# Token tiles laid down the image, with conv1, conv2 and the output transposes handed on chunk by chunk

## The chip, the core and the metric

One core of a Trainium2 chip runs the whole program in one launch. The metric is the device time in microseconds, as the median of several runs. TensorE (PE) multiplies and transposes, VectorE (DVE), ScalarE (ACT) and GpSimd (POOL) work on elements, SyncE (SP) issues the DMAs.

## The reference

Eight images x of 64 x 64 pixels and 48 channels go through four layers, all in float32:

```
L0: attention over all 4096 tokens of an image, then concat with x (96 channels),
    1x1 conv + leaky ReLU ("conv1"), 3x3 conv + leaky ReLU ("conv2"), 1x1 conv ("w3"), + x
L1: ReLU, 3x3 depthwise conv, 1x1 conv, batch norm
L2: routing (mean, 4 experts), 1x1 conv to 192 ("expand"), 3x3 depthwise, 1x1 conv to 48 ("project")
L3: as L1
```

## The kernel before

The images are pipelined. One iteration f of the loop does conv2, w3 and L1 of image f, project and L3 of image f-1 (`back`), and attention and conv1 of image f+1 (`attn`). Iterations 0 and 7 are written out, 1 to 6 are a loop, each image takes 142.3 us. Everything is ordered by hand: each engine has its own program, and semaphores tie them together. TensorE's order in an iteration is conv2, project(0), w3(3), project(1), l1(0,1), project(2,3), transposes of x, l1(2), l1(3), attention scores, routing, l3 (four chunks), attention sums, `out_tokens` (16 transposes), attention weights, halo of the expansion, and conv1 with the expansions between its chunks.

**Two layouts.** Convolutions work on "pairs": a partition holds one of 2 x 48 channels (even and odd row of a row pair), the free axis holds rows and columns; a PSUM bank is 512 elements, 8 rows of 64. Attention works on "tokens": `tok` has 128 tokens on the partitions, in 16 tiles i for each row parity. Before, tile i takes columns 16q + i (q = 0 to 3, `WQ`) of all 32 row pairs, so every token tile spans the whole height of the image. A group of four transposed tiles (a chunk of 512 tokens) is therefore four columns out of each quarter, all rows of one parity.

**conv1** runs over 8 such chunks k. TensorE transposes four tiles (L1045) and multiplies (L1053), ScalarE copies the input (L1279) and writes 0.2 times the result to y1 (L1286), VectorE takes the maximum twice: L670 into the float32r tile y1_h in image layout, and L672 back into y1. GpSimd then subtracts (L949) for y1_l, VectorE does the last chunk itself (L676). L670 reads bank and y1 in the order of the image: runs of 4 elements, 128 apart (`bank_tokens`, `y1_tokens`), and writes through `y1_view`. The two banks of ring C are freed by L672 (y1_max). In the loop an expansion (L1109, L1110) stands between conv1's chunks, whose result ScalarE (L1377) or VectorE (L648) takes.

**conv2** (L1070) does 27 matmuls for each of 8 chunks of 8 rows. Its first matmul waits for all eight y1_h chunks, its 19th for all y1_l chunks, because a chunk of tokens spans all rows.

**w3_out** (L702) adds w3's bank, a bias and x, which it reads from xcm with a stride of 128.

**l3** (L1094 to L1097) does 15 matmuls for each of four chunks, ScalarE evacuates them to outc (L1362). After the attention sums `out_tokens` transposes outc, tile i being outc[:, i::16] (L1172), and ScalarE copies four groups to ot (L1370). Ring D's two banks are taken in turn; place p waits for the reader of place p - 2.

**DMAs.** `load_x` issues 12 DMAs an image (pieces of 192 bytes), `store` 4, with runs of 3072 bytes on both sides. VectorE's depthwise convolution of an image waits until the store before has landed, since ot shares its tile.

## Time and profile before

| | us |
|---|---|
| median of 3 runs (1265.3 to 1267.52) | 1265.95 |
| the profiled run | 1266.09 |
| its span | 1264.3 |
| TensorE busy | 1175.6 |
| VectorE busy | 892.4 |
| ScalarE busy | 475.6 |
| GpSimd busy | 119.8 |

The span is that of one execution taken by the profiler. "PE" is a matmul, "PEld" a weight load beside it. In the tables of groups a row gives line, engine, operation, output and inputs, shapes, count, then busy time and mean ns, then idle time before it and what ended it. In the timeline the first two columns are start and duration in us, and the brackets hold the idle time before and its cause. Matmuls are pipelined, so one may be shown 0.4 us long while the next starts 0.24 us after it.

### The profile page before, as it was taken

The page shows a single profiled execution, that of the slowest core. Times are in us where ns is not written, and L with a number is a line of the kernel's source. Part 1 is how long each engine was busy: PE and PEld are TensorE (multiplying, and loading weights), DVE is VectorE, ACT ScalarE, POOL GpSimd, SP SyncE. Part 2 cuts the span into 40 slices and gives each one's busy share as a digit, 9 for nine tenths or more (in the row PEclk, how much of TensorE's full clock was granted, in tenths as well). Part 3 has the DMA queues.
Part 4 walks back from the last instruction along what each step waited for, and adds up shares of the span by engine and source line. Part 5 has one row for each costly group of instructions (what it writes and reads, how often), then busy time and mean ns, then how long its engine had stood idle before and what let it go on. Part 6 is the DMA issues. An engine that isn't in the chain of part 4 may idle for free.

```text
span 1264.3 us, 14703 instructions
## 1 busy us (share of the span) xinstructions
PE 1175.6 (93%) x4981; PEld 756.8 (60%) x4981; DVE 892.4 (71%) x1154; ACT 475.6 (38%) x812; POOL 119.8 (9%) x72
## 2 busy tenths in 40 slices
PE   4789879999999999999999999999999999998986
PEld 3556566646665575656665575656665575655434
DVE  4552359984699459984699459984699459982850
ACT  3211334245532444245532444245532444242421
POOL 0310003000300003000300003000300003000000
PEclk9689869999999999999999999999999999999997
DMA  2011631069113772069113771069113770069016
GB/s 52 21 36 21 81 51 38 1 85 132 45 21 40 100 103 37 0 85 131 44 21 40 100 103 37 0 85 130 45 22 40 101 103 1 1 85 134 25 27 83
DMA packets 183179, 72.91 MB, mean 58 GB/s; under 512 B 174349, under 2 KB 174962, under 8 KB 183154
## 3 DMA queue, kind: packets, MB, share of 16 engines
q1 hardware_dynamic: 183154, 72.58, 41.6%
q8 instruction: 15, 0.25, 0.1%
q14 instruction: 10, 0.08, 0.0%
HBM read 10.51 MB, written 6.29 MB: 13 GB/s over the span
## 4 chain that ended last, share of the span: by engine, by line
PE 80%; DVE 7%; issue 4%; ACT 3%; SPq 2%; DMA 2%; POOL 0%; ACTq 0%; DVEq 0%; POOLq 0%
PE bank L1070 32%; PE bank L1094 8%; PE bank L1024 4%; PE bank L1081 4%; PE bank L1053 4%; PE bank L1160 3%; PE bank L1161 3%; PE bank L1013 3%; DVE dwa L632 3%; PE bank L1097 3%; PE bank L1096 3%; PE bank L1109 2%; PE bank L1138 2%; PE bank L1110 2%; DMA y_parts<-a_parts 2%
## 5 line engine op out<-in xcount | busy, mean ns | idle before, releaser
L1070 PE MATMUL bank<-y_parts,w_h 96*96 96x512 f32 x1152 | 301.8, 411 | 0.0
L632 DVE SCALAR_TENSOR_TENSOR dwa<-h1a,dyn,dwa 128x1024 f32<-128x1024 f32 x240 | 294.0, 1278 | 0.0
L1070 PEld LDWEIGHTS bank<-y_parts,w_h 96*96 96x96 f32 x1152 | 186.6, 163 | 98.5 <-issue 13.2
L632 DVE SCALAR_TENSOR_TENSOR dwb<-h1b,dyn,dwb 128x1024 f32<-128x1024 f32 x128 | 154.9, 1278 | 0.0
L1070 PE MATMUL bank<-y_parts,w_l 96*96 96x512 f32 x576 | 147.9, 401 | 0.0
L1094 PE MATMUL bank<-a_parts,wt_h 128*96 128x512 f32 x384 | 117.4, 415 | 16.4 <-DMA y_parts<-a_parts 15.9
L1070 PEld LDWEIGHTS bank<-y_parts,w_l 96*96 96x96 f32 x576 | 93.4, 162 | 44.3
L949 POOL TENSOR_TENSOR y_parts<-y,y_parts 96x512 fp32r<-96x512 f32 x56 | 96.4, 1725 | 190.5 <-DVE y L672 189.0
L943 POOL TENSOR_TENSOR tok<-tok,u 128x1536 f32<-128x1536 f32 x8 | 22.4, 2796 | 747.3 <-DVE u L573 747.3
L1094 PEld LDWEIGHTS bank<-a_parts,wt_h 128*96 128x96 f32 x384 | 61.5, 166 | 49.6 <-issue 18.7
L713 DVE SCALAR_TENSOR_TENSOR a_parts<-v,a_parts 96x512 fp32r<-96x512 f32 x64 | 43.5, 688 | 52.4 <-ACT a_parts L1339 49.6
L1053 PE MATMUL bank<-xq,w_cur 97*96 97x512 f32 x128 | 69.5, 625 | 9.7 <-DVE y L672 9.7
L670 DVE TENSOR_TENSOR y_parts<-bank,y 96x512 fp32r<-96x512 f32 x64 | 68.5, 1071 | 7.6 <-ACT y L1286 6.7
L1311 ACT ACTIVATE y<-bank,b2s 96x512 f32<-96x512 f32 x32 | 21.9, 683 | 136.3 <-PE bank L1070 136.3
L1311 ACT ACTIVATE xq<-bank,b2s 96x512 f32<-96x512 f32 x32 | 21.9, 685 | 130.9 <-PE bank L1070 122.0
L1024 PE MATMUL bank<-tok 128*97 128x48 f32 x512 | 55.0, 277 | 15.6 <-POOL tok L943 15.6
L1160 PE MATMUL bank<-dwa,pc 128*96 128x512 f32 x128 | 65.4, 592 | 0.0
L1161 PE MATMUL bank<-dwb,pc 128*96 128x512 f32 x128 | 65.3, 592 | 0.0
L1024 PEld LDWEIGHTS bank<-tok 128*97 128x97 f32 x512 | 55.0, 196 | 16.9 <-issue 16.0
L726 DVE TENSOR_TENSOR y_parts<-y,y_parts 96x512 fp32r<-96x512 f32 x32 | 22.1, 689 | 50.8 <-ACT y_parts L1352 50.8
L1094 PE MATMUL bank<-a_parts,wt_l 128*96 128x512 f32 x192 | 57.8, 410 | 0.0
L1362 ACT ACTIVATE dwa<-bank,conv_bias,inv 96x512 f32<-96x512 f32 x32 | 24.8, 774 | 81.4 <-PE bank L1097 81.4
(223 smaller groups left out, 1701.6 us busy)
## 6 DMA issues: line engine op xcount, KB each, us to landing
y_parts<-a_parts SPq DMA_DIRECT2D x32, 396.0 KB, 6.1
y_parts<-a_parts SPq DMA_DIRECT2D x64, 192.0 KB, 6.6
tok<-in_x_dram SPq DMA_DIRECT2D x96, 96.0 KB, 2.6
a_parts<-a_parts SPq DMA_DIRECT2D x32, 264.0 KB, 3.3
x_even<-y_parts SPq DMA_DIRECT2D x16, 384.0 KB, 9.0
x_odd<-y_parts SPq DMA_DIRECT2D x16, 384.0 KB, 7.9
out_dram<-dwb SPq DMA_DIRECT2D x32, 192.0 KB, 2.3
y_parts<-a_parts SPq DMA_DIRECT2D x32, 132.0 KB, 4.3
```

Of the source, the lines that this page charges most:

```text
L632: nc.vector.scalar_tensor_tensor(out=dst, in0=tap_input(n, t), scalar=weight, in1=dst, op0=ALU.mult, op1=ALU.add).then_inc(tap_step, 1)
L670: nc.vector.tensor_tensor(y1_view(y1_h, k - 1), bank_tokens(bank), y1_tokens(k - 1), ALU.max).then_inc(y1h_ready, 1)
L713: return nc.vector.scalar_tensor_tensor(out=lo[:, rows, 1:W + 1], in0=src[:, m % 2, :].rearrange("p (j w) -> p j w", w=W), scalar=0.0, in1 ...
L949: nc.gpsimd.tensor_tensor(y1_view(y1_l, k), y1_tokens(k), y1_view(y1_h, k).bitcast(F32), ALU.subtract).then_inc(y1l_ready, 1)
L1024: last = nc.tensor.matmul(bank[0:SUMS, 0:C], token(par, i, X_AT, SUMS), token(par, i, K_AT, C), start=first, stop=final)
L1053: nc.tensor.matmul(bank[0:C2, :], w1_cur[:, :], xq[:, (k - 1) % 2, :], start=True, stop=True)\
L1070: last = nc.tensor.matmul(bank[0:C2, :], wgt[:, t, :], src[:, rows, cols], start=t + n == 0, stop=t == TAPS - 1 and n == 2)
L1081: last = nc.tensor.matmul(bank[0:C2, :], w3eo[:, par, :], rows[:, :, par, :], start=par == 0, stop=par == 1)
L1094: nc.tensor.matmul(bank[0:C2, :], wgt[layer][:, kw, :], own[:, rows, kw:kw + W], start=n + kw == 0, stop=False)
L1160: nc.tensor.matmul(bank[0:C2, :], pc[:, 0, cols], first[:, :, par, :], start=False, stop=False)
L1161: last = nc.tensor.matmul(bank[0:C2, :], pc[:, 1 + m // 2, cols], other[:, :, par, :], start=False, stop=par == 1)
L1311: nc.scalar.activation(y2[(k // 2) % 2][:, (k % 2) * BANK:(k % 2 + 1) * BANK], ring_c.bank(C_2 + k)[0:C2, :], ACT.Identity, bias=b2s[:, 0: ...
```

## The change

The token tiles are laid out differently: tile i takes rows 4i to 4i + 3, all 64 columns, two row pairs (`STEP` = 2) by 64 columns on 128 partitions. Four tiles of one parity are then eight rows of that parity, and four tiles of pairs are exactly one bank of the pair layout. From this follow:

- L670, L676, L949 and L702 read and write plain rows; the gather patterns go. VectorE no longer waits for L670 before L672.
- conv1's chunk k is parity k % 2 of rows 16(k // 2) to 16(k // 2) + 15, so rows are finished from the top.
- conv2's chunk k waits for y1_h and y1_l of chunks up to k + 1 only. ScalarE, which writes y2 over y1 at k = 2, waits there for all low parts.
- `out_tokens` transposes tile by tile the chunk that l3 has made. TensorE's order is l3(0), l3(1), out(0), l3(2), out(1), l3(3), out(2), attention sums, out(3). Ring D's places follow: l3 has 4, 5, 7, 9, the transposes 6, 8, 10, 11. ScalarE copies in the same order.
- `load_x` is 6 DMAs of 64 partitions, `store` 4 DMAs of 64 partitions; both sides of each in pieces of 192 bytes (48 channels of one pixel).

The diff, with what is left out marked:

```diff
-WQ = 4
-RUN = W // WQ
+STEP = 2
+RUN = PAIRS // STEP
-X_LOADS = 3 * WQ
+X_LOADS, STORES = 3 * STEP, 2 * STEP
...
-        D_P, D_L3, D_OUT = 0, 4, 8
+        D_P, D_L3, D_OUT = 0, (4, 5, 7, 9), (6, 8, 10, 11)
         ring_d = Ring(banks[6:8], [(ah3_ready, PCHUNKS, n + 1) for n in range(PCHUNKS)]
-                      + [(outc_ready, PCHUNKS, n + 1) for n in range(PCHUNKS)]
-                      + [(ot_ready, 4, n + 1) for n in range(4)], first_free=True)
+                      + [(outc_ready, PCHUNKS, 1), (outc_ready, PCHUNKS, 2), (ot_ready, 4, 1), (outc_ready, PCHUNKS, 3),
+                         (ot_ready, 4, 2), (outc_ready, PCHUNKS, 4), (ot_ready, 4, 3), (ot_ready, 4, 4)], first_free=True)
...
         def y1_tokens(k):
 
-            return columns(y1[:, :, :], (k % Y1_BUFFERS) * BANK, [[WQ, PAIRS], [1, WQ], [128, 4]])
-
-        def bank_tokens(bank):
-            return columns(bank, 0, [[WQ, PAIRS], [1, WQ], [128, 4]])
+            return y1[:, k % Y1_BUFFERS, :].rearrange("p (j w) -> p j w", w=W)
 
         def y1_view(tile, k):
 
-            par, i0 = k // 4, 4 * (k % 4)
-            return columns(tile[:, :, :], (1 + par) * WP + 1 + i0, [[2 * WP, PAIRS], [RUN, WQ], [1, 4]])
+            r0 = 1 + 2 * ROWS * (k // 2) + k % 2
+            return tile[:, r0:r0 + 2 * ROWS - 1:2, 1:W + 1]
...
-                    nc.vector.tensor_tensor(y1_view(y1_h, k - 1), bank_tokens(bank), y1_tokens(k - 1), ALU.max).then_inc(y1h_ready, 1)
-                    dve.wait_ge(y1h_ready, CHUNKS * image + k)
+                    nc.vector.tensor_tensor(y1_view(y1_h, k - 1), bank.rearrange("p (j w) -> p j w", w=W), y1_tokens(k - 1), ALU.max).then_inc(y1h_ready, 1)
...
-                x_in = columns(xcm[0:C2, :], m * ROWS * WQ, [[1, ROWS * WQ], [128, RUN]])
                 nc.vector.scalar_tensor_tensor(
-                    out=v[:, m % 2, :].rearrange("p (a b) -> p a b", b=RUN),
-                    in0=ring_b.bank(B_W3 + m)[0:C2, :].rearrange("p (a b) -> p a b", b=RUN),
-                    scalar=col0[:, Z_B3:Z_B3 + 1], in1=x_in, op0=ALU.add, op1=ALU.add).then_inc(v_ready, 1)
+                    out=v[:, m % 2, :], in0=ring_b.bank(B_W3 + m)[0:C2, :], scalar=col0[:, Z_B3:Z_B3 + 1],
+                    in1=xcm[0:C2, m * BANK:(m + 1) * BANK], op0=ALU.add, op1=ALU.add).then_inc(v_ready, 1)
...
-            for n in range(2 * WQ):
-                par, q = n % 2, n // 2
-                sp.dma_start(tok[q::WQ, par, :, X_AT:X_AT + C], src[par, q]).then_inc(x_loaded, 16)
-            for q in range(WQ):
-                sp.dma_start(tok[q::WQ, 1, :, Q_AT:Q_AT + C], src[0, q]).then_inc(x_loaded, 16)
+            for par, at, of in ((0, X_AT, 0), (1, Q_AT, 0), (1, X_AT, 1)):
+                for j in range(STEP):
+                    sp.dma_start(tok[j * W:(j + 1) * W, par, :, at:at + C], src[of, j]).then_inc(x_loaded, 16)
...
-            dst = out[image].rearrange("(j b) (q i) c -> q j b (i c)", b=2, q=WQ)
-            for q in range(WQ):
-                sp.dma_start(dst[q], ot[q::WQ, :].rearrange("p (b n) -> p b n", b=2)).then_inc(stored, 16)
+            dst = out[image].rearrange("(i j b) w c -> j b w i c", j=STEP, b=2)
+            for j in range(STEP):
+                src = ot[j * W:(j + 1) * W, :].rearrange("p (b i c) -> p b i c", b=2, c=C)
+                for par in range(2):
+                    sp.dma_start(dst[j, par], src[:, par]).then_inc(stored, 16)
...
-                        par, i0 = k // 4, 4 * (k % 4)
+                        par, i0 = k % 2, 4 * (k // 2)
...
-                        if k == 0 and n == 0:
-                            pe.wait_ge(y1h_ready, CHUNKS * image + CHUNKS)
-                        if k == 0 and n == 2:
-                            pe.wait_ge(y1l_ready, POOL_CHUNKS * image + POOL_CHUNKS)
+                        if n == 0 and k + 2 <= CHUNKS:
+                            pe.wait_ge(y1h_ready, CHUNKS * image + k + 2)
+                        if n == 2 and k + 2 <= POOL_CHUNKS:
+                            pe.wait_ge(y1l_ready, POOL_CHUNKS * image + k + 2)
+                        if n == 2 and k + 2 == CHUNKS:
                             pe.wait_ge(y1l_last, image + 1)
...
-            def out_tokens(image):
-                for n in range(4):
-                    bank = ring_d.take(pe, image, D_OUT + n)
-                    if n == 0:
-                        pe.wait_ge(outc_ready, PCHUNKS * image + PCHUNKS)
+            def out_tokens(image, chunks):
+                for n in chunks:
+                    bank = ring_d.take(pe, image, D_OUT[n])
+                    pe.wait_ge(outc_ready, PCHUNKS * image + n + 1)
                     for m in range(4):
                         i = 4 * n + m
-                        last = nc.tensor.transpose(bank[:, m * C2:(m + 1) * C2], outc[:, i::RUN], ident[0:C2, 0:C2])
+                        last = nc.tensor.transpose(bank[:, m * C2:(m + 1) * C2], outc[:, i * 128:(i + 1) * 128], ident[0:C2, 0:C2])
                     last.then_inc(outt_done, 1)
...
+            def l3_and_out(image):
+                l3(image, (0, 1))
+                for m in range(2, PCHUNKS):
+                    out_tokens(image, (m - 2,))
+                    l3(image, (m,))
+                out_tokens(image, (PCHUNKS - 2,))
...
+                    if k == 2:
+                        act.wait_ge(y1l_ready, POOL_CHUNKS * (f + 1))
+                        act.wait_ge(y1l_last, f + 1)
...
+            def l3_and_tokens_out(b, chunks):
+                for m in chunks:
+                    l3_out(b, (m,))
+                    tokens_out(b, (m - 1,))
...
                 if back is not None:
-                    l3_out(back, (0, 1))
+                    l3_out(back, (0,))
+                    l3_and_tokens_out(back, (1,))
                 if attn is not None:
                     root_of_q(attn)
                 if back is not None:
-                    l3_out(back, (2, 3))
-                    tokens_out(back)
+                    l3_and_tokens_out(back, (2, 3))
+                    tokens_out(back, (PCHUNKS - 1,))
```

## Rows read from the trace of the kernel before

**Rows 1.** The page, busy time of each engine.
```profile
PE 1175.6 (93%) x4981; PEld 756.8 (60%) x4981; DVE 892.4 (71%) x1154; ACT 475.6 (38%) x812; POOL 119.8 (9%) x72
```
**Rows 2.** Waits of TensorE, 205 to 1145: total us, times, longest.
```profile
PE bank L1159 <- ACT dwa L1302: 7.6, 7, 1.2
```
**Rows 3.** Groups by line and form, VectorE.
```profile
L670 DVE TENSOR_TENSOR y_parts<-bank,y 96x512 fp32r<-96x512 f32 x64 | 68.5, 1071 | 7.6 <-ACT y L1286 6.7
L672 DVE TENSOR_TENSOR y<-bank,y 96x512 f32<-96x512 f32 x64 | 44.0, 687 | 2.2
...
L702 DVE SCALAR_TENSOR_TENSOR v<-bank,col,xcm 96x512 f32<-96x512 f32 x32 | 35.7, 1117 | 11.5 <-PE bank L1081 11.5
...
L690 DVE SCALAR_TENSOR_TENSOR y<-bank,col,y 96x512 f32<-96x512 f32 x32 | 23.8, 745 | 20.6 <-ACT y L1311 20.6
```
**Rows 4.** Stages, conv1: length, busy PE, PEld, DVE, ACT, POOL, granted clock, DMA.
```profile
467.40:488.88 21.48, 19.99 (x88) 12.09 (x86) 17.56 (x25) 13.45 (x25) 11.54 (x7) 1.00 0.19 55
```
**Rows 5.** Timeline, TensorE in the conv1 stage of that image.
```profile
476.41 1.09 PE L1053 MATMUL bank<-xq,w_cur 97*96 97x512 f32 x2 [0.38 <-DVE y L672]
...
485.71 1.09 PE L1053 MATMUL bank<-xq,w_cur 97*96 97x512 f32 x2 [0.70 <-DVE y L672]
...
488.72 2.38 PE L1070 MATMUL bank<-y_parts,w_h 96*96 96x512 f32 x9
```
**Rows 6.** Chain that ended last, one chunk of that stage: start, us, what.
```profile
478.41 0.86 PE bank L1053 x2
479.27 0.24 PE bank L1109
479.51 0.23 PE bank L1110
479.75 0.44 PE bank L1045 x4
```
**Rows 7.** Timeline, output transposes of that image, and those of the tail.
```profile
464.80 2.35 PE L1172 MATMUL bank<-ident,dwa 96*128 96x96 f32 x16
...
465.12 0.20 DVE L597 TENSOR_TENSOR gm<-bank,gram_mask 97x48 f32<-97x48 f32 x1
...
467.07 0.37 PE L1032 MATMUL bank<-wva_aug,gt 97*48 97x96 f32 x2
...
1256.71 2.37 PE L1172 MATMUL bank<-ident,dwa 96*128 96x96 f32 x16 [0.96 <-ACT dwa L1362]
```
**Rows 8.** Timeline, from w3 of the last pair to project(2).
```profile
551.20 1.09 DVE L702 SCALAR_TENSOR_TENSOR v<-bank,col,xcm 96x512 f32<-96x512 f32 x1 [1.23 <-PE bank L1081]
...
563.62 0.47 PE L1159 MATMUL bank<-x_even,pick 96*96 96x512 f32 x1 [1.09 <-ACT dwa L1302]
```
**Rows 9.** Timeline, TensorE in the prologue.
```profile
17.84 2.47 PE L1001 MATMUL bank<-ident,tok 128*96 128x128 f32 x10 [2.88 <-DMA tok<-in_x_dram]
...
56.39 1.10 PE L1053 MATMUL bank<-xq,w_cur 97*96 97x512 f32 x2 [0.63 <-DVE y L672]
...
63.60 1.10 PE L1053 MATMUL bank<-xq,w_cur 97*96 97x512 f32 x2 [0.76 <-DVE y L672]
...
68.64 0.79 PE L990 MATMUL bank<-col,h1a 48*96 48x1 f32 x4 [3.45 <-DVE colm L509]
...
69.36 4.16 PE L1070 MATMUL bank<-y_parts,w_h 96*96 96x512 f32 x9
```
**Rows 10.** Stages as above: first load, then SBUF copies; last, DMA share and GB/s.
```profile
9.00:17.00 8.00, 3.05 (x12) 1.98 (x12) 3.33 (x17) 0.00 (x0) 0.00 (x0) 1.00 0.75 145
446.00:458.00 12.00, 12.00 (x52) 8.17 (x51) 11.22 (x22) 6.38 (x8) 2.80 (x1) 1.00 1.42 143
```
**Rows 11.** Timeline, the end of the last iteration and the last store.
```profile
1215.41 2.25 ACT L1302 ACTIVATE dwa<-dwa 128x1024 f32<-128x1024 f32 x2 [1.76 <-DVE dwa L632]
...
1220.15 0.80 PE L1159 MATMUL bank<-x_even,pick 96*96 96x512 f32 x1
...
1259.69 2.52 SPq L870 DMA_DIRECT2D out_dram<-dwb  x4
```

More of the change, by code:

```diff
@@ L621, in depthwise @@
                     if s == 0:
-                        after(dve, stored, 16 * WQ * image)
+                        after(dve, stored, 16 * STORES * image)
                         dve.wait_ge(h1b_ready, H1B_WRITES * (image + 1))
@@ L1082, in w3, with pair_conv @@
                 last.then_inc(w3_done, 1)
-            def pair_conv(image, layer, ring, first, done, chunks):
+            def pair_conv(image, layer, ring, places, done, chunks):
                 for m in chunks:
-                    bank = ring.take(pe, image, first + m)
+                    bank = ring.take(pe, image, places[m])
                     if m % 2 == 0:
@@ L1176, in l1, with l3 @@
                 pair_conv(image, L1, ring_b, B_L1, l1_done, chunks)
[L1178 to L1179 removed]
+            def l3(image, chunks):
+                pair_conv(image, L3, ring_d, D_L3, l3_done, chunks)
+            def l3_and_out(image):
[4 more added lines that the diff above has]
+                out_tokens(image, (PCHUNKS - 2,))
             def iteration(f, attn, back):
```

31 lines of the change are left out of this document (15 added, 16 removed).

## The prediction

> **What bounds the kernel now.** I read the page first: TensorE is busy 93% of the span, VectorE 71% [rows 1]. So the kernel is TensorE's queue, and only two things can move the time: TensorE idling less, or the head and tail where no matmul runs. The waits of TensorE inside the loop come next. From 205 to 1145 us, six and a half images, the largest is 7.6 us for a ReLU that closes a depthwise chain [rows 2]; the next ones are in conv1, 0.38 and 0.70 us in the image read here, for VectorE's second max L672 [rows 5]. Then the timeline of one image (142.3 us) by stages. In conv1 (467.4 to 488.9) TensorE is busy 19.99 of 21.48 us, VectorE 17.56, ScalarE 13.45, GpSimd 11.54 [rows 4]. conv2's first matmul starts at 488.72 and shows no wait, though the code makes it wait for all eight chunks [rows 5]. So the chunkwise waits of conv2 have nothing to give by themselves: TensorE runs its queue in order, and what is queued before conv2 ends just as late. What can move conv2 is conv1's own pace.
>
> **VectorE's strided operations.** L670 reads bank and y1 in runs of 4 elements 128 apart and takes 1071 ns; L672, the same size read in a row, takes 687 [rows 3]. After the change L670 reads as L672 does: 0.69 us, 0.38 less. L676 reads the same pattern and I give it the same 0.4. L702 (1117) becomes the form of L690 (745): 0.37 less. GpSimd (L949) also reads in a row from now on; even unchanged, 11.54 us for seven chunks [rows 4], it fits.
>
> **conv1, per image in the loop.** From the third conv1 matmul (476.41) to the eighth (485.71) are five chunks, 1.86 us each [rows 5]. VectorE needs 1.07 + 0.69 and about 0.1 between, 1.86, so it sets the pace; TensorE's own work for a chunk is 0.86 (conv1) + 0.24 + 0.23 (expansion) + 0.44 (four transposes) = 1.77 [rows 6]. With VectorE at 1.48 TensorE sets it. The third matmul comes 0.39 earlier (its wait is 0.38), each next gains 0.09, and the wait of 0.70 before the eighth shrinks, since L672 two chunks back ends 0.4 + 0.36 earlier. After that ScalarE (L1286, then L1377, for whose bank the last expansion waits) still follows the eighth matmul by the same steps. I get the eighth at 484.6 and conv2 at 487.5: 1.2 us less, for seven images 8.4 us. Bounds: 0.4 (only the third matmul, ScalarE takes over at 1.86) to 1.5 (all idle of the stage).
>
> **conv2 and project.** conv2 itself has no wait. TensorE stands 1.09 us at 563.62, at the end of a chain that begins when w3 of the last pair is done (551.20, VectorE had been idle 1.23) with L702 [rows 8]. Only L702's 0.37 counts in it, whatever VectorE gained before: 0.4 less, in seven images (2.6 us). ScalarE's new wait at k = 2 sits ahead of y2, some 20 us after the last low part: nothing. In image 0 L702 also lies before the copies that TensorE waits for: 0.4.
>
> **The output transposes.** Here the change adds waits. Before, l3's four chunks run without a pause, then the attention sums, then 16 transposes from 464.80 to 467.07 [rows 7]. Now chunk 2 of l3 takes a bank whose reader is the evacuation of chunk 1, just finished; chunk 3 likewise. The row of the tail gives the price, since there the transposes wait for exactly such an evacuation: TensorE idles 0.96 [rows 7], and 0.16 more in which the matmul before, shown 0.40 long at a spacing of 0.24, would have been overlapped: 1.12 us from slot to slot. A group of four transposes, 0.47 (2.35 for 16, less a wait of 0.3 and the overlap), fills a part of it; the rest, 0.65, is idle. Queued behind it are l3, the sums, the weights and the whole conv1 stage. The sums start 1.12 + 1.12 + 0.47 = 2.71 later (the third group stands behind chunk 3). Behind the sums one group is left, and attention_weights needs VectorE's gt and gm, which end 0.52 after 464.80 and release TensorE 0.14 later [rows 7]: the weights come 0.66 behind the sums, not 2.27. 2.71 + 0.66 - 2.27 = +1.1 us an image, six images +6.6. It is nothing if the stops don't occur, and 1.4 if no group fills any of them. In the last iteration and at the tail all 16 transposes waited for ScalarE already: two stops 2.24, then 1.6 instead of 3.4 (tail: 2.15 instead of 4.0, the last copy included): +0.5 and +0.4.
>
> **Prologue.** conv1 of image 0 has no expansions; its odd chunks form a chain from 56.39 to 63.60, 3.60 us per two [rows 9], with one L670 in it. Four links of 0.38 and L676's 0.35 in front of colm: -1.8 us. If GpSimd holds 1.7 per chunk against the new 1.6, 0.8 of it is lost.
>
> **DMAs.** load_x goes from 12 issues to 6 of the same 192-byte pieces, 6144 in all. The issues take 8 us now, and the data flow at 145 GB/s at a share of 0.75 [rows 10]: full use would be 193 GB/s, 6.1 us for 1.18 MB; copies in SBUF with 256-byte pieces run at 143 GB/s [rows 10], 8.3 us. Data begin at about 8.9 and 7.2 us, the middle, bring TensorE's start to about 16.6, not 17.84 [rows 9]: -1.2, between -1.9 and, if the scattered reads take 12 us, +2.2. In the loop the load is hidden by 80 us. The store now writes 4096 pieces of 192 bytes instead of 256 of 3072. Now it is 4 issues in 2.52 us at 1259.69 [rows 11]. No row shows such a store; the nearest are the load (4.1 us at 193 GB/s) and the SBUF copies (28.6 ns per piece and engine, 7.3 us). I take the middle, 5.7: +3.1, bounds +1.5 and +4.8, and +9.7 if each piece costs the copies' full packet time (1.42 x 12 us x 16 engines over about 6000 pieces, 46 ns). In the loop this hides behind conv1. In the last iteration VectorE waits for the store before its depthwise; it starts when the old store has just landed, and its first ReLU ends 1216.5 while TensorE wants it at 1220.15 [rows 11]: 3.7 us of cover, 4.0 with the 0.5 above. Beyond 4.0 each us counts twice.
>
> **Sum.** Profiled run 1266.09 (span 1264.3 and 1.8 around it; the median is 1265.95). Load -1.2, conv1 of image 0 -1.8, image 0's L702 -0.4, seven conv1 stages -8.4, seven project waits -2.6, six transposes +6.6, last iteration +0.5, tail +0.4, store +3.1: -3.8, so 1262.3.
>
> **Rivals.** (a) Forecast: 1262.3, its own range 1259.5 to 1265; chance 0.40.
>
> (b) The clock stays up. TensorE runs conv2's first nine matmuls of image 0 in 4.16 us after an idle of 3.45 [rows 9], and in 2.38 in the loop, where the granted clock of the stage ahead is 1.00 [rows 4, 5]. The pause shrinks to about 2.8. If that keeps the 2.4 GHz level, 1.8 to 2.0 more goes: 1260.4. Against it: the short transposes in the pause were there before. Chance 0.12.
>
> (c) ScalarE takes VectorE's place in conv1. For: it is busy 13.45 us for eight chunks, 1.68 each against TensorE's 1.77 [rows 4, 6], so small gaps between its three operations a chunk would make it the pace at 1.86 again. Against: it idles in the stage today. Then a stage gives 0.4, seven lose 5.6: 1267.9. Chance 0.20.
>
> (d) The small pieces decide, and it is slower. Place: the store at the tail and the one VectorE waits for in the last iteration. Price: 256 pieces per engine times t, minus 2.6, counted again beyond 4.0. At t = 46 ns it is 9.2 at the tail and 5.2 in the last iteration against 3.1: 1273.6. It is slower than 1268.6 from t = 36 ns on. For: the copies in SBUF show that packet time. Against: they overlap there, and the load's pieces show 16 ns. Chance 0.17.
>
> (e) Each piece is moved twice: 8.2 us, +5.6 at the tail, +1.6 in the last iteration, 1266.4. For: small pieces are written here for the first time to HBM. Against: the load of equal pieces shows nothing of it. Chance 0.11. The Trainium skill, "DMA: Bandwidth & Descriptors", Specifications, says that below 512 bytes a DMA engine reads, modifies and writes; by it the store crosses that line and doubles, and no row here shows a small write to HBM.
>
> That the change doesn't do what it says is true of one part: conv2's chunk waits. It is in the forecast, at zero.
>
> **Numbers.** Within 0.2% (about what a measurement of this kernel can tell from no change) is 1263.5 to 1268.5. Faster: 0.32 of (a), (b): 0.45 with rounding. Same: the rest of (a), most of (c), (e): 0.34. Slower: (d) and a little of (c): 0.21. The range 1258 to 1271 takes (a), (b), (c), (e) and the mild half of (d).
>
> **What would show it.** L670 at about 0.69 and L702 at 0.75; conv1 chunks 1.77 apart, no wait of L1053 for L672; conv1 in 20.3 us. TensorE waits of about 0.6 us twice in l3 for L1362. The wait at L1159 at 0.7. The first transpose near 16.6; last store issue to end of span 3 us longer. The prediction is wrong if l3 shows no stops (6 us better), if ScalarE paces conv1, or if the store takes over 9 us.

## The result, and the profile after

| | us |
|---|---|
| before, median of 4 runs beside it | 1266.09 |
| changed, median of 4 runs (1258.3 to 1259.41) | 1259.01 |
| ratio, 95% interval | 0.9943 (0.9931 to 0.9954) |
| span of the profiled run, before and changed | 1264.3, 1257.6 |

One of the six executions of experiment 4 took 4018.53 us, a slow run of unknown cause; its ratio leaves it out.

The changed kernel is 7.1 us faster (0.6%); the forecast was 3.7 us (1262.3 against 1265.95). So the gain is nearly twice the one forecast, and 1259.01 lies 0.5 below the range of the forecast's own case (a), 1259.5 to 1265; it is inside the wider range only. The page of the changed kernel, busy time of each engine, beside [rows 1]:

```profile
PE 1168.3 (93%) x4981; PEld 754.2 (60%) x4981; DVE 849.4 (68%) x1154; ACT 473.0 (38%) x812; POOL 90.4 (7%) x72
```

VectorE lost 43 us of work and GpSimd 29, as plain rows are read faster. TensorE lost 7.3, about what the span lost. The waits of TensorE inside the loop (total us, times, longest), 205 to 1145, beside [rows 2]:

```profile
PE bank L1154 <- ACT dwa L1303: 7.7, 7, 1.2
PE bank L1089 <- ACT dwa L1366: 6.4, 12, 0.5
...
PE bank L1047 <- DVE y L668: 2.3, 6, 0.4
```

The second row is new: two stops of l3 (now L1089) for its evacuation, in each of six images. The wait for VectorE's second max, 6.6 us before in the same stretch, is down to 2.3. The first row, from which I had expected 2.6 us, has not moved; experiment 6 shows why.

Groups by form, to be read beside [rows 3] (L667, L668, L697 are L670, L672, L702 of before):

```profile
L667 DVE TENSOR_TENSOR y_parts<-bank,y 96x512 fp32r<-96x512 f32 x64 | 44.0, 687 | 25.8 <-ACT y L1287 25.7
L668 DVE TENSOR_TENSOR y<-bank,y 96x512 f32<-96x512 f32 x64 | 43.3, 677 | 0.0
L697 DVE SCALAR_TENSOR_TENSOR v<-bank,col,xcm 96x512 f32<-96x512 f32 x32 | 23.7, 742 | 17.0 <-PE bank L1076 17.0
L943 POOL TENSOR_TENSOR y_parts<-y,y_parts 96x512 fp32r<-96x512 f32 x56 | 67.1, 1199 | 210.1 <-DVE y L668 210.1
L1166 PEld LDWEIGHTS bank<-ident,dwa 96*128 96x128 f32 x128 | 13.9, 142 | 5.7 <-ACT dwa L1366 1.6
```

L667 and L697 take what was forecast, 0.69 and 0.74. The last row is one that I had not looked for: outc is loaded as the stationary operand of the output transposes. The same group in the kernel before, which read every 16th column:

```profile
L1172 PEld LDWEIGHTS bank<-ident,dwa 96*128 96x128 f32 x128 | 15.7, 204 | 5.2 <-ACT dwa L1362 2.8 <-ACT dwb L1370 2.4
```

**conv1.** The stage of the same image, columns as in [rows 4], and three of its steps in TensorE's timeline, beside [rows 5]:

```profile
463.20:483.59 20.39, 19.61 (x89) 12.26 (x89) 14.16 (x25) 13.59 (x25) 8.32 (x7) 1.00 0.33 61
```
```profile
475.63 1.02 PE L1047 MATMUL bank<-xq,w_cur 97*96 97x512 f32 x2
...
477.39 1.02 PE L1047 MATMUL bank<-xq,w_cur 97*96 97x512 f32 x2
...
480.58 1.09 PE L1047 MATMUL bank<-xq,w_cur 97*96 97x512 f32 x2 [0.38 <-DVE y L668]
...
483.01 0.50 PE L1104 MATMUL bank<-x_odd,ew_h 96*128 96x512 f32 x1 [0.41 <-ACT h1a L1386]
...
483.59 2.38 PE L1065 MATMUL bank<-y_parts,w_h 96*96 96x512 f32 x9
```

The chunks are 1.76 us apart, TensorE's own pace; the wait before the eighth has shrunk from 0.70 to 0.38, the one for ScalarE has stayed. conv2 follows the attention weights (463.16) by 20.43 us, against 21.65 before (467.07 to 488.72): 1.22 less.

**l3 and the output transposes**, TensorE's timeline, beside [rows 7]:

```profile
447.46 0.49 PE L1166 MATMUL bank<-ident,dwa 96*128 96x96 f32 x4
448.48 0.95 PE L1089 MATMUL bank<-a_parts,wt_h 128*96 128x512 f32 x3 [0.53 <-ACT dwa L1366]
...
456.80 0.49 PE L1166 MATMUL bank<-ident,dwa 96*128 96x96 f32 x4
457.13 5.62 PE L1018 MATMUL bank<-tok 128*97 128x48 f32 x64
462.58 0.52 PE L1166 MATMUL bank<-ident,dwa 96*128 96x96 f32 x4
463.16 0.37 PE L1026 MATMUL bank<-wva_aug,gt 97*48 97x96 f32 x2
```

A stop is 1.02 us from slot to slot (forecast 1.12), of which the group of four transposes, 0.33 where nothing waits (456.80 to 457.13), fills a third. The weights come 0.58 us behind the last group.

**Where the 6.7 us of the span went.** conv2's first matmul of each image is a mark that both traces have. Differences, changed less before, in us:

| stretch | before | changed | difference | forecast |
|---|---|---|---|---|
| start to conv2 of image 0 | 69.36 | 67.39 | -1.97 | -3.0 |
| iteration 0 | 134.91 | 133.27 | -1.64 | -1.6 |
| six iterations of the loop | 853.46 | 848.82 | -4.64 | -2.8 |
| last iteration, to l3 of the last image | 180.90 | 180.09 | -0.81 | +0.1 |
| l3 and transposes at the tail | 20.98 | 21.20 | +0.22 | +0.4 |
| store | 4.69 | 6.83 | +2.14 | +3.1 |
| sum | | | -6.70 | -3.8 |

Only the rows of the loop and of the store can be read to a tenth. Ten traces of kernels whose instructions are the same up to there start their first transpose between 17.40 and 17.94 us, and iteration 0 takes 132.8 to 134.4 us in the ten kernels with the changed kernel's conv1 and w3_out. The other rows are single differences of two traces. That iteration 0 came out as forecast (-1.64 against -1.6) is therefore partly luck.

### The profile page after: what moved, and what is told of

It is laid out like the page before. It is cut to its first block, busy times and chain, and to the rows that moved or that the text cites. A ratio compares the mean times of both kernels' runs of the same rounds, so it can differ in the third digit from the quotient of the medians.

```text
span 1257.6 us, 14703 instructions
## 1 busy us (share of the span) xinstructions
PE 1168.3 (93%) x4981; PEld 754.2 (60%) x4981; DVE 849.4 (68%) x1154; ACT 473.0 (38%) x812; POOL 90.4 (7%) x72
## 4 chain that ended last, share of the span: by engine, by line
PE 81%; DVE 6%; ACT 4%; issue 4%; DMA 2%; SPq 2%; POOL 0%; ACTq 0%; DVEq 0%; POOLq 0%
PE bank L1065 32%; PE bank L1089 9%; PE bank L1018 4%; PE bank L1076 4%; PE bank L1047 4%; DVE dwa L629 3%; PE bank L1007 3%; PE bank L1155 3%; PE bank L1156 3%; PE bank L1092 3%; PE bank L1091 3%; PE bank L1104 3%; PE bank L1133 2%; PE bank L1105 2%; PE bank L1039 2%
## 5 line engine op out<-in xcount | busy, mean ns | idle before, releaser
L1089 PE MATMUL bank<-a_parts,wt_h 128*96 128x512 f32 x384 | 120.9, 424 | 23.3 <-DMA y_parts<-a_parts 14.8
L1089 PEld LDWEIGHTS bank<-a_parts,wt_h 128*96 128x96 f32 x384 | 60.8, 166 | 54.5 <-issue 20.0
L943 POOL TENSOR_TENSOR y_parts<-y,y_parts 96x512 fp32r<-96x512 f32 x56 | 67.1, 1199 | 210.1 <-DVE y L668 210.1
L667 DVE TENSOR_TENSOR y_parts<-bank,y 96x512 fp32r<-96x512 f32 x64 | 44.0, 687 | 25.8 <-ACT y L1287 25.7
L1089 PE MATMUL bank<-a_parts,wt_l 128*96 128x512 f32 x192 | 57.6, 409 | 0.0
```

What stands on the lines that cost most here:

```text
L667: nc.vector.tensor_tensor(y1_view(y1_h, k - 1), bank.rearrange("p (j w) -> p j w", w=W), y1_tokens(k - 1), ALU.max).then_inc(y1h_ready, 1)
L943: nc.gpsimd.tensor_tensor(y1_view(y1_l, k), y1_tokens(k), y1_view(y1_h, k).bitcast(F32), ALU.subtract).then_inc(y1l_ready, 1)
L1089: nc.tensor.matmul(bank[0:C2, :], wgt[layer][:, kw, :], own[:, rows, kw:kw + W], start=n + kw == 0, stop=False)
```

## The experiments

Most were made from the changed kernel. Medians stand beside runs of the kernel before on the same chip. "An image" is the mean distance of conv2's first matmul over the six iterations of the loop: 142.24 us before, 141.47 changed.

**1. The order of before around l3.** Layout, load and store stay changed.

```diff
-        D_P, D_L3, D_OUT = 0, (4, 5, 7, 9), (6, 8, 10, 11)
+        D_P, D_L3, D_OUT = 0, (4, 5, 6, 7), (8, 9, 10, 11)
...
-                    l3_and_out(back)
+                    l3(back, range(PCHUNKS))
...
-                    out_tokens(back, (PCHUNKS - 1,))
+                    out_tokens(back, range(PCHUNKS))
...
```

The readers of ring D's places and ScalarE's order go back too, and l3 and the transposes at the tail likewise. A group of transposes still waits for its own chunk only, not for all four as before; that matters where no attention sums stand between.

> The changed kernel with the order of before around l3: four chunks of l3, attention sums, 16 output transposes; ring D's places and ScalarE's order as before. Layout, load and store stay changed. My theory (the two stops of about 0.5 us idle, 1.02 us from slot to slot, are pure loss): the block from l3 to the attention weights gets 0.83 us shorter in each of six images (5.0 us), the last iteration stays within 0.1, the tail gains 0.2. From 1259.0 to about 1253.8. Rival (the stops only move TensorE's wait for VectorE's gt and for ScalarE from behind the sums to in front of them): within 1 us of 1259.0. In the trace: no wait of l3 for L1366, attention weights 7.7 us behind the start of the sums.

1251.38 us (five executions, 1250.84 to 1254.85), ratio 0.9890 (0.9876 to 0.9904); an image takes 140.33. The transposes of the same image:

```profile
458.29 0.84 PE L1166 MATMUL bank<-ident,dwa 96*128 96x96 f32 x8
...
459.38 0.93 PE L1166 MATMUL bank<-ident,dwa 96*128 96x96 f32 x8 [0.25 <-ACT dwb L1379]
...
460.24 0.37 PE L1026 MATMUL bank<-wva_aug,gt 97*48 97x96 f32 x2
```

The rival falls: the stops are pure loss. But they cost 1.14 us an image, not 0.83. I had taken 0.83 from the two traces (the block from l3 to the weights grew by that much), and that difference already holds a gain: here the 16 transposes and their pause take 1.95 us, 0.32 less than the 2.27 of the kernel before in the same order (464.80 to 467.07 [rows 7]). The rest of the 7.6 us is not the order's alone: of 8.7 us between the two spans 6.8 are the loop, 0.6 the head, where the order plays no part, and 1.2 what follows. At the tail two things are mixed. l3's matmuls ran short 3.3 us after their start instead of 5.6 (the granted clock was 0.50 until then and 1.00 after), but a wait of 0.66 us for a copy came in behind. Experiment 9 has the same order and a clock that rose as late as the changed kernel's (0.50 for the first 5.4 us in both): from l3's first matmul to the first issue of the store it takes 20.25 us, the changed kernel 21.29. So the alternating order costs 1.0 us at the tail as well, not the 0.2 that I had expected.

**2. The stride of the transposes, and the store of before.** Experiment 1 with

```diff
-                    pe.wait_ge(outc_ready, PCHUNKS * image + n + 1)
+                    pe.wait_ge(outc_ready, PCHUNKS * image + PCHUNKS)
...
-                        last = nc.tensor.transpose(bank[:, m * C2:(m + 1) * C2], outc[:, i * 128:(i + 1) * 128], ident[0:C2, 0:C2])
+                        last = nc.tensor.transpose(bank[:, m * C2:(m + 1) * C2], outc[:, i::RUN], ident[0:C2, 0:C2])
...
-            dst = out[image].rearrange("(i j b) w c -> j b w i c", j=STEP, b=2)
+            dst = out[image].rearrange("(j b) (q i) c -> q j b (i c)", b=2, q=4)
...
```

> The order of before around l3, and the output transposes read every 16th column of outc again, and the store is that of before to the letter (4 DMAs, pieces of 3072 bytes); pixels land in the wrong places, so the output is not the reference's. Of the changed kernel conv1, conv2's waits, w3_out and the load are left. Theory (a weight load of a strided outc takes 205 ns instead of 141): the transposes between the sums and the weights take 2.27 us again, not 1.95, an image of the loop 140.66 us instead of 140.34; from the last copy to the end 4.7 us instead of 6.8. Together 1251.4 + 1.9 - 2.1 = 1251.2. Rival (the 0.32 is due to the transposes' place in time, not their stride): 140.34 an image, 1249.3.

1251.68 us, ratio 0.9886 (0.9870 to 0.9903). (Unlike what the expectation says, nothing is misplaced: outc is in the order of the image, so this is the whole output path of before.) An image takes 140.66, 0.33 more than in experiment 1, and the weight load 204 ns again:

```profile
L1164 PEld LDWEIGHTS bank<-ident,dwa 96*128 96x128 f32 x128 | 15.7, 204 | 5.2 <-ACT dwa L1364 2.8 <-ACT dwb L1377 2.4
```
```profile
458.28 2.35 PE L1164 MATMUL bank<-ident,dwa 96*128 96x96 f32 x16
460.56 0.37 PE L1024 MATMUL bank<-wva_aug,gt 97*48 97x96 f32 x2
```

The 16 transposes and their pause take 2.28 us again (458.28 to 460.56), as before. So the stride of the weight load is worth 0.33 us an image in this order. The rival of the expectation, their place in time, falls, since the place is that of experiment 1. In the changed kernel's order the stride was not undone; there the two groups inside a stop leave 0.53 idle, which a slower group would fill first.

**3. VectorE's pattern in conv1.**

```diff
-                    nc.vector.tensor_tensor(y1_view(y1_h, k - 1), bank.rearrange("p (j w) -> p j w", w=W), y1_tokens(k - 1), ALU.max).then_inc(y1h_ready, 1)
+                    nc.vector.tensor_tensor(y1_view(y1_h, k - 1).rearrange("p j (a i) -> p j a i", i=4), columns(bank, 0, [[16, 8], [1, 16], [128, 4]]),
+                                            columns(y1[:, :, :], buffer * BANK, [[16, 8], [1, 16], [128, 4]]), ALU.max).then_inc(y1h_ready, 1)
+                    dve.wait_ge(y1h_ready, CHUNKS * image + k)
```

> The changed kernel, but L667 (y1_h) reads bank and y1 with the pattern of before (runs of 4 elements, 128 apart) and VectorE waits again between L667 and L668. It writes plain rows, so the 512 pixels of a chunk land permuted: the output is not the reference's, the work is the same. My theory (VectorE set the pace of conv1 at 1.86 us): L667 takes 1.07 us again, a conv1 chunk 1.86, the stage 21.5 instead of 20.4, seven times 1.2 = 8.4 us, and in the prologue another 1.5 to 2.3: 1259.0 to about 1269. Rival (the gain in conv1 comes as much from GpSimd, 1.20 instead of 1.73 us, and from L672, which stay fast here): 1263 to 1265.

1269.79 us, ratio 1.0020 (1.0011 to 1.0029): slower than before. An image takes 142.70, 1.23 more than the changed kernel, and L667 1059 ns. GpSimd still takes 1.20 us here (1200 ns), and the gain is gone all the same: the rival falls, VectorE's pace is the cause, by its pattern and its wait together (experiment 5 takes the wait alone). In image 0 it all comes back too: from the attention sums' first matmul to conv2 it is 33.18 us, 33.19 before and 30.89 changed.

**4. The bank alone.** As 3, with y1 in a row and no wait.

```diff
-                                            columns(y1[:, :, :], buffer * BANK, [[16, 8], [1, 16], [128, 4]]), ALU.max).then_inc(y1h_ready, 1)
-                    dve.wait_ge(y1h_ready, CHUNKS * image + k)
+                                            y1_tokens(k - 1).rearrange("p j (a i) -> p j a i", i=4), ALU.max).then_inc(y1h_ready, 1)
```

> As the run above, but only the PSUM bank is read with the old pattern, y1 in a row, and without VectorE's wait (again a permuted output). If the pattern costs as soon as one operand has it, L667 takes 1.07 us, VectorE needs 1.76 a chunk against TensorE's 1.77, the pace stays and only the waits at the third and eighth matmul return: 0.6 us in seven stages and 1.5 us in the prologue, 1259.0 to about 1264.7. If the cost is that of the SBUF operand, L667 stays at 0.69 and nothing moves. Between them the costs add up, 0.88 us, and the time is about 1261.

1259.31 us, ratio 0.9942 (0.9929 to 0.9955); an image 141.47. L667 in experiment 3, then here:

```profile
L667 DVE TENSOR_TENSOR y_parts<-bank,y 96x512 fp32r<-96x512 f32 x64 | 67.8, 1059 | 8.6 <-ACT y L1289 5.5
```
```profile
L667 DVE TENSOR_TENSOR y_parts<-bank,y 96x512 fp32r<-96x512 f32 x64 | 44.0, 687 | 25.8 <-ACT y L1288 25.7
```

The PSUM operand read with jumps of 128 elements costs nothing here. The 0.37 us come with the SBUF operand. y1 alone with jumps and without the wait was not tried, since L668 would overwrite what L667 still reads, but w3_out is such a case: in experiment 6 only its SBUF operand jumps, its bank is read in a row, and it takes 1119 ns against 742. The Trainium skill, "Vector Engine (DVE) Microarchitecture Reference", section 5.2, gives 1.73 ns a column where one source hops at every element and 1.054 where all is contiguous. By an estimate from these two figures that is 1.64 times; here the two whole operations are 1.54 (1059 by 687) and 1.51 times (1119 by 742).

**5. The wait alone, and the load in 12 DMAs**, two edits in one kernel, far apart in time, and a single execution.

```diff
+                    dve.wait_ge(y1h_ready, CHUNKS * image + k)
...
-                    sp.dma_start(tok[j * W:(j + 1) * W, par, :, at:at + C], src[of, j]).then_inc(x_loaded, 16)
+                    for half in range(2):
+                        p0 = half * W // 2
+                        sp.dma_start(tok[j * W + p0:j * W + p0 + W // 2, par, :, at:at + C], src[of, j][p0:p0 + W // 2]).then_inc(x_loaded, 16)
```

> The changed kernel, with two separate edits: VectorE's wait between L667 and L668 is back, and x comes in 12 DMAs of 32 partitions instead of 6 of 64. Read from the profile. Wait: VectorE then needs about 1.5 us a chunk against TensorE's 1.77, so an image of the loop takes 141.5 us as without it (the stride alone is what cost 1.2); rival: up to 0.5 of the 1.2 come back. Load: if the number of issues rules, the first transpose comes at 17.8 as before the change, if the data rate (155 GB/s) does, at 17.5.

An image takes 141.73, 0.26 more: of the 1.23 us of experiment 3 the wait alone makes 0.26, and the other 0.97 come only with the jumps. My "nothing" was wrong by that. In image 0 the wait makes 0.5 (from the sums' first matmul to conv2 31.36 against 30.89). Two rows of VectorE, first of the changed kernel, then of this one, show what it costs: L667's partner starts 0.61 us behind it there, and 0.73 here.

```profile
480.94 0.69 DVE L667 TENSOR_TENSOR y_parts<-bank,y 96x512 fp32r<-96x512 f32 x1 [0.49 <-ACT y L1287]
481.55 0.68 DVE L668 TENSOR_TENSOR y<-bank,y 96x512 f32<-96x512 f32 x1
```
```profile
484.06 0.69 DVE L667 TENSOR_TENSOR y_parts<-bank,y 96x512 fp32r<-96x512 f32 x1 [0.37 <-ACT y L1290]
484.79 0.69 DVE L669 TENSOR_TENSOR y<-bank,y 96x512 f32<-96x512 f32 x1
```

That is 0.12 where TensorE waits for the bank, at the third and eighth matmul. The first transpose comes earlier than in any trace with six DMAs (17.32 to 17.94 in twelve):

```profile
16.99 3.75 PE L998 MATMUL bank<-ident,tok 128*96 128x128 f32 x16 [1.96 <-DMA tok<-in_x_dram]
```

Its single time, 1263.71, is 4.3 us above the changed kernel's profiled run. 1.6 are the wait, and 2.9 more lie in iteration 0 (136.17 against 133.27): there w3's last four matmuls took 3.70 us instead of 1.93. The granted clock was 0.50 from 130 to 135 us (the lower level, 1.2 GHz), against 0.78 in the changed kernel, and l1 then waited 1.71 us for a halo copy.

**6. w3_out.**

```diff
-                    out=v[:, m % 2, :], in0=ring_b.bank(B_W3 + m)[0:C2, :], scalar=col0[:, Z_B3:Z_B3 + 1],
-                    in1=xcm[0:C2, m * BANK:(m + 1) * BANK], op0=ALU.add, op1=ALU.add).then_inc(v_ready, 1)
+                    out=v[:, m % 2, :].rearrange("p (a b) -> p a b", b=RUN),
+                    in0=ring_b.bank(B_W3 + m)[0:C2, :].rearrange("p (a b) -> p a b", b=RUN),
+                    scalar=col0[:, Z_B3:Z_B3 + 1], in1=columns(xcm[0:C2, :], m * 32, [[1, 32], [128, RUN]]),
+                    op0=ALU.add, op1=ALU.add).then_inc(v_ready, 1)
```

> The changed kernel, but L697 (w3_out) reads xcm with a stride of 128 as before; the pixels it adds are the wrong ones, so the output is not the reference's, the work is the same. My theory: L697 takes 1.12 us instead of 0.74 and the 0.37 comes back once an image in front of l1 and project(2): seven images and image 0, 3.0 us, 1259.0 to 1262.0. Rival (the wait at project(2) did not shrink in the changed kernel, 7.7 against 7.6 us, so L697 was no part of it): within 0.6 us of 1259.0.

1261.81 us, ratio 0.9960 (0.9947 to 0.9974); an image 141.83, 0.36 more, L697 1119 ns. The theory holds, in size and in place. Two rows of the changed kernel's timeline (l1's first weight load, project's first matmul), and the same two of this run:

```profile
549.34 0.16 PEld L1089 LDWEIGHTS bank<-a_parts,wt_h 128*96 128x96 f32 x1 [0.27 <-issue]
...
558.14 0.47 PE L1154 MATMUL bank<-x_even,pick 96*96 96x512 f32 x1 [1.09 <-ACT dwa L1303]
```
```profile
549.52 0.16 PEld L1091 LDWEIGHTS bank<-a_parts,wt_h 128*96 128x96 f32 x1 [0.27 <-issue]
...
558.68 0.47 PE L1156 MATMUL bank<-x_even,pick 96*96 96x512 f32 x1 [1.44 <-ACT dwa L1305]
```

Measured from conv2 of the same image (483.59 and 483.77), l1 starts at 65.75 us in both, and project(2) at 74.55 and 74.91. So the whole 0.36 comes back at the wait that I had named, 1.44 instead of 1.09. Why that wait did not shrink between the kernel before and the changed one shows l1's first weight load before:

```profile
555.16 0.48 PEld L1094 LDWEIGHTS bank<-a_parts,wt_h 128*96 128x96 f32 x3 [0.95 <-DMA y_parts<-a_parts]
```

There l1 starts 66.44 us after conv2 and waits for its halo copies, the changed kernel's l1 0.69 earlier. But project(2) stands behind a chain of VectorE and ScalarE that does not depend on l1's start: it comes at 74.90 before (563.62 [rows 8] less 488.72) and at 74.55 changed, as much earlier as L697 is shorter. l1's earlier start therefore only gives TensorE more to wait for at project(2), which hides the gain from the list of waits. l1's wait is absent in experiment 6 and in experiment 3 as well; the kernel before has the slower conv1 and the slower w3_out together. Its going is worth nothing.

**7. conv2's waits for all chunks.**

```diff
-                        if n == 0 and k + 2 <= CHUNKS:
-                            pe.wait_ge(y1h_ready, CHUNKS * image + k + 2)
-                        if n == 2 and k + 2 <= POOL_CHUNKS:
-                            pe.wait_ge(y1l_ready, POOL_CHUNKS * image + k + 2)
-                        if n == 2 and k + 2 == CHUNKS:
+                        if k == 0 and n == 0:
+                            pe.wait_ge(y1h_ready, CHUNKS * image + CHUNKS)
+                        if k == 0 and n == 2:
+                            pe.wait_ge(y1l_ready, POOL_CHUNKS * image + POOL_CHUNKS)
```

> The changed kernel, but conv2's first matmul waits for all eight y1_h chunks and its 19th for all low parts, as before. My theory: TensorE's queue puts every conv1 matmul ahead of conv2, so nothing moves, 1259.0 within 0.6, and conv2's first matmul still shows no wait in the loop. Rival: part of the gain came from conv2 starting before the last low part was ready: then up to 0.7 us (one VectorE operation, L672 of the changed kernel) comes back per image, 1263.9, and the 19th matmul shows a wait.

1259.48 us, ratio 0.9943 (0.9930 to 0.9956), an image 141.47. No matmul of conv2 is in the list of waits of the loop, and the first shows none:

```profile
482.87 0.40 PE L1104 MATMUL bank<-x_odd,ew_l 96*128 96x512 f32 x1
483.10 2.38 PE L1064 MATMUL bank<-y_parts,w_h 96*96 96x512 f32 x9
```

So conv2's chunkwise waits, which the title names, are worth nothing.

**8. Sizes of the pieces.** Three kernels, with the store's `dst` laid out in pieces of 16, 4 or 2 tiles. The first also reads x from contiguous pieces; the second issues the 324 KB weight load only when x has landed. The second and the third are single executions.

```diff
-            dst = out[image].rearrange("(i j b) w c -> j b w i c", j=STEP, b=2)
+            dst = out[image].rearrange("h w c -> (h w c)").rearrange("(j b i w n) -> j b w i n", j=STEP, b=2, w=W, n=16 * C)
...
```

> The changed kernel with the same 6 load and 4 store DMAs, but on the DRAM side each partition's data lie in one piece of 3072 bytes (wrong pixels, so the output is not the reference's; the SBUF side stays as it is). My theory for the store: the end of the program, from the last copy to ot to the end of the span, falls from 6.8 to about 4.7 us, as before the change, and VectorE's wait of 1.84 us for the store in the last iteration goes without moving the end. For the load: if the scattered reads are what holds it at 155 GB/s, TensorE's first transpose comes at about 16.6 instead of 17.5 us; if not, it stays. So 1259.0 to 1256.0 (both) or 1256.9 (store alone). Rival for the store: the issue of four DMAs with more descriptors is what takes longer, then the time falls by less than 1 us.

> The changed kernel, but the store writes pieces of 768 bytes (four tiles together, wrong places, so the output is not the reference's), 1024 pieces instead of 4096; and the 324 KB weight load is issued only when x has landed. Read from the profile. If the store's price goes with the number of pieces (2.1 us for 3840 more), the end takes 4.7 + 0.4 = 5.1 us; if a threshold at 512 bytes is what counts, it takes 4.7, as with 3072. Load: if the weight load shares the engines with x, the first transpose comes about 1 us earlier, 16.5; if not, it stays at 17.5.

> The changed kernel, but the store writes pieces of 384 bytes (two tiles together, wrong places, so the output is not the reference's), 2048 pieces. Read from the profile. By the number of pieces the end takes 4.7 + 1.0 = 5.7 us; if every piece below 512 bytes is read, changed and written back, moving each byte twice, it takes as long as with 192, 6.8, for bytes rather than pieces count.

The first gave 1258.9 us, ratio 0.9927 (0.9914 to 0.9941), the others 1257.56 and 1257.26. The first's median is only 0.1 below the changed kernel's, where I had expected 2 to 3 us; its five executions lie from 1256.65 to 1259.33, and its profiled span is 1.3 shorter. What the pieces cost is therefore read from the end of the traces alone. The last store's issue in the timelines of the changed kernel, then of pieces of 3072, 768 and 384 bytes:

```profile
1250.86 3.43 SPq L864 DMA_DIRECT2D out_dram<-dwb  x4
```
```profile
1250.87 2.45 SPq L864 DMA_DIRECT2D out_dram<-dwb  x4
```
```profile
1249.78 2.86 SPq L864 DMA_DIRECT2D out_dram<-dwb  x4
```
```profile
1248.82 3.21 SPq L864 DMA_DIRECT2D out_dram<-dwb  x4
```

From the start of that issue to the end of the span (1257.6, 1256.3, 1255.7, 1255.2) it is

| piece, bytes | 3072 | 768 | 384 | 192 |
|---|---|---|---|---|
| us | 5.4 | 5.9 | 6.4 | 6.7 |

This stretch repeats well: seven traces with the store of 192-byte pieces give 6.73 to 6.75. So 1.3 of the 2.1 us are the small pieces. The other 0.8 lie between the contiguous run and the store of before, 4.61 (1259.69 to 1264.3 [rows 11]) and 4.58 in experiment 2, whose DMAs take every fourth partition instead of 64 neighbours; in the traces a piece of 3072 bytes keeps its DMA engine busy 202 ns in the one shape and 126 in the other, and why was not taken apart. The expectation of 4.7 was wrong by these 0.8. The steps, 0.5, 0.5 and 0.3, show no jump between 768 and 384 bytes, and they do not grow with the number of pieces either. An engine is busy 55.5 ns with a piece of 768 bytes, 28.2 with 384 and 15.4 with 192: 0.072, 0.073 and 0.080 ns a byte. The Trainium skill, "DMA: Bandwidth & Descriptors", Specifications, puts a read-modify-write below 512 bytes. If that moved each byte twice, 384 would stand with 192 and apart from 768, and these runs do not show it.

For the load: with contiguous source pieces the first transpose starts at 17.52, with the weight load held back at 17.32, in the changed kernel at 17.53. Neither the scattered reads nor the neighbour holds it by the 1 us that I had looked for; the differences are no larger than those between traces with the same load (17.40 to 17.94).

**9. Two queues for the last store**, from experiment 1: the DMAs of j = 0 from SP, those of j = 1 from ScalarE.

```diff
-            store(sp, IMAGES - 1)
+            store(sp, IMAGES - 1, (0,))
...
             tokens_out(IMAGES - 1, range(PCHUNKS))
+            store(act, IMAGES - 1, (1,))
```

> The order of before around l3 everywhere, and the last image's four store DMAs from two queues, two from SP, two from ScalarE, all at the end. If one queue's issue time (3.4 us for four) is what makes the end long, 1.5 us go: 1251.4 to 1249.9. If the writing of 4096 small pieces is, less than 0.4 goes.

1251.87 us, ratio 0.9888 (0.9872 to 0.9905): nothing. The issue takes half as long, the end comes no sooner:

```profile
1242.62 1.36 SPq L867 DMA_DIRECT2D out_dram<-dwb  x2
1242.62 1.66 ACTq L867 DMA_DIRECT2D out_dram<-dwb  x2
```

The span ends at 1249.7, 7.1 us behind it, where experiment 1 has 6.7. The transfer is what lasts, not its issue; a piece keeps its engine busy 17.2 ns here and 15.4 there.

**10. The version that the runs point to.** The order of before in the loop; at the tail the order of the change, with the store in two halves.

```diff
+            sp.wait_ge(ot_ready, 4 * IMAGES - 2)
+            store_half(sp, IMAGES - 1, 0, range(STEP))
+            sp.wait_ge(ot_ready, 4 * IMAGES)
+            store_half(sp, IMAGES - 1, 1, (0,))
...
+            act.wait_ge(ot_ready, 4 * IMAGES)
+            store_half(act, IMAGES - 1, 1, (1,))
```

> The kernel with the order of before around l3 in the loop and in the last iteration; only for the last image l3 and the transposes alternate, and its store goes in two halves: tiles 0 to 7 of every partition as soon as two chunks are copied (four DMAs from SP, beside l3's last chunks), tiles 8 to 15 at the end, two DMAs from SP and two from ScalarE. Theory (the tail's 6.7 us are 3.4 of issue on one queue and 3.3 behind the last issue, and half the pieces are gone by then): from the last copy to the end about 1.7 + 2.8 = 4.5 us, 2.2 less; the two stops in the tail cost 0.8 of it. So 1.0 to 1.4 below the run with the order of before alone (1251.4): about 1250.2. Rival (what is behind the last issue does not depend on how much is written): 1251.4 or more.

1248.67 us, ratio 0.9865 (0.9848 to 0.9881). The last issue and the end (1246.4) are 4.4 us apart instead of 6.7:

```profile
1241.99 1.56 ACTq L878 DMA_DIRECT2D out_dram<-dwb  x2
```

It beats both kernels, the one before by 17.8 us. The time is 2.7 below experiment 1, where 1.0 to 1.4 were expected. The end gave 2.3 of it, about as reckoned. But the last image's l3 also came 0.9 earlier after its conv2 (179.38 against 180.30), which the edit doesn't explain, and the alternating tail cost only 0.2 (20.01 us against 19.85 from l3's first matmul to the last issues), beside a run that had its own wait of 0.66 there. So the 2.3 is shown, the rest is not.

## Why the prediction was right, and where it was not

**The loop** is accounted for, if the parts add up. From 140.33 (experiment 1) the way back to 142.24 is the strided transposes 0.33, w3_out 0.36, conv1's pattern and wait 1.23: 142.25. For the changed kernel:

| an image of the loop | forecast | runs |
|---|---|---|
| conv1 | -1.2 | -1.23 |
| w3_out | -0.37 | -0.36 |
| order around l3 | +1.1 | +1.14 |
| outc read in a row | none | -0.33 |
| conv2's waits | 0 | 0 |
| sum | -0.47 | -0.78 |

The missing line is the failed step of the sum. I had priced the four groups at what a group took before (0.47) and looked for strided reads on VectorE only. In the part on the output transposes I wrote down 2.35 us for 16 without asking what they read. Over six images it is 1.8 us.

That the order came out at 1.1 is luck in part. The forecast compared the new block with strided transposes, 2.27 us behind the sums; the run without the alternation takes 1.95 there. That makes the order dearer by 0.32, and the two stops, the third group and the weights, all shorter than I had put them, make it cheaper by 0.28. Read straight from the traces of the two kernels, the block from l3 to the weights grew by 0.82, not 1.1: the third group took 0.33 instead of 0.47, the weights come 0.58 instead of 0.66 behind the sums' last group, and each stop is some hundredths shorter. conv1 and w3_out came true by the mechanism forecast: VectorE's pace, TensorE's own pace of 1.76 after it, and the wait at project(2).

**The last iteration** was put at +0.5 for the order; from the marks above, -0.81 less w3_out's 0.36 leaves -0.45. The stops are there, but the groups beside them are short, the wait of 0.96 for ScalarE behind l3 became 0.62, and a wait of 0.24 for a copy in the middle of l3, present before, is gone: from l3's first matmul to the end of this part both kernels need the same within 0.1 us. l3's wait for its copies, 1.99 before, was 1.52; what made it shorter was not looked into.

**The store** came at +2.1, inside my bounds of 1.5 and 4.8 and a us below the middle that I took. The small pieces were only 1.3 of it: 0.8 came from the shape of the DMAs, which I had not costed. The 2.6 us that the forecast takes off for the old store stands on no row of it. Its 46 ns for a piece was high too: 6776 pieces were in that stretch, not about 6000, which makes 40, and a piece of the store took 15.4. VectorE waited 1.8 us for the store in the last iteration:

```profile
DVE dwb L625 <- DMA out_dram<-dwb: 1.8, 1, 1.8
```

With contiguous pieces it waits 0.5, and l3 of the last image still starts at the same distance from conv2 (180.47 against 180.09). The cover of 3.7 us held. Rivals (d) and (e) fall with that. The page named beside (e) gives no price; that it doubles the store was my reading of it.

**The head** was over-forecast by 1.0, as far as two traces tell. Rows of the changed kernel beside [rows 9]:

```profile
17.53 3.75 PE L995 MATMUL bank<-ident,tok 128*96 128x128 f32 x16 [2.47 <-DMA tok<-in_x_dram]
21.11 7.44 PE L1007 MATMUL bank<-qkw,xcm 97*128 97x192 f32 x32
36.50 10.66 PE L1018 MATMUL bank<-tok 128*97 128x48 f32 x64 [7.95 <-POOL tok L937]
...
66.97 0.49 PE L984 MATMUL bank<-col,h1a 48*96 48x1 f32 x4 [2.64 <-DVE colm L506]
```

The load gave 0.3 between these two, not 1.2, and that is within what traces of the same load differ by; nothing is shown to be gained. Its data run at 168 GB/s between 9 and 16 us, below the 193 that I had reckoned. With x alone in the queues, 6 GB/s are left from 16 us on, and the transposes start at 17.32: about a us lies between the last byte and the engine, where my sum had half a us. Then the scores (L1007) took 7.44 us, 6.81 before, at a granted clock of 1.00 in both. They take 6.25 to 7.47 in the traces of kernels whose instructions there are the same, so this is no effect of the change; what it is stays open. From 36.50 to conv2 it is 30.89 against 33.19, so conv1 gave 2.3, more than the 1.8 forecast. The 0.5 that lack are the wait between L670 and L672, which I had left out of these links: experiment 5 puts it back and gets 31.36.

**Rival (b)** did not come true: conv2's first nine matmuls took 3.75 us, not 4.16, at a granted clock of 0.74 instead of 0.62 from 66 to 70 us, far from the 2.38 of the loop. Nor is the shorter pause shown to be the reason for the 0.4: in experiment 1 the pause is as short (2.65 against 2.64) and they take 4.16. **Rival (c)** fell: ScalarE is busy 13.59 us in the stage and TensorE waits for it once, 0.41, as before.

## What to carry to other kernels

When a layout changes, list every reader of the tile with its stride, weight loads included, and price each from its own row. A wait that is loosened where the engine shows no wait gives nothing, and an order that alternates producer and consumer on two banks buys a stop for every bank it hands over at once. If the size of a gain is taken from two traces, undo one part at a time: the 0.83 read here was 1.14 less about 0.32. And a wait that keeps its length is no proof that nothing was gained in front of it: measure from a fixed mark to the instruction that waits.

## What the runs showed of the hardware

- VectorE, 96 x 512 float32: an SBUF operand read in jumps of 128 elements makes 742 ns into 1119 (experiment 6) and, with a PSUM bank read so too, 687 into 1059 (experiment 3); the PSUM bank alone costs nothing (687, experiment 4).
- A weight load of 96 x 128 float32 takes 142 ns from a row and 204 with a step of 16 elements; GpSimd's subtraction takes 1199 ns in a row and took 1725 in the gather pattern of before.
- A store of 786 KB takes, from the start of its issue to the end of the program, 5.4 to 6.7 us for pieces of 3072 to 192 bytes, with no jump between 768 and 384, and 4.6 us for pieces of 3072 bytes from every fourth partition. Halving the issue time on two queues takes nothing off it, halving the bytes left at the end (with two queues) 2.3 us.
- In the one trace with x in 12 DMAs of 32 neighbouring partitions the first transpose starts at 16.99 us, in twelve traces with 6 DMAs of 64 at 17.32 to 17.94.
- Head and tail differ by a us and more where the instructions are the same. At the tail of experiment 1 l3's matmuls were 0.24 us apart after 3.3 us, in the changed kernel after 5.6 (0.43 until then, at a granted clock of 0.50); experiment 9, with experiment 1's order, was as late as the changed kernel. In experiment 5 an early fall to the 1.2 GHz level stood beside a loss of 2.9 us in iteration 0. Differences of a us at the ends are therefore no evidence. An image of the loop agrees within 0.02 us between kernels with the same loop.
